# A two-layer cross-attention and feed-forward kernel: the second layer's queries made ahead of its loop for four batches and two heads at once, kept in DRAM, and one value phase a unit

## The reference

```
q_hk = (hidden_q @ Wq.T).reshape(Bv, Sv, H, K)               # 16 heads of 128
q_big = jnp.einsum('bshk,hkq->bshq', q_hk, w_kc_q)           # to 192
q_big = _apply_rope(q_big, sin_q[None, :, None, :], cos_q[None, :, None, :])
kv_r = _apply_rope(kv_c, sin_k[None], cos_k[None])           # 1444 rows of 64 a batch
q_r = jnp.einsum('bshq,hqr->bhsr', q_big, W_qr)              # to 64
k_r = jnp.einsum('bld,hdr->bhlr', kv_r, W_kr)
scores = jnp.einsum('bhsr,bhlr->bhsl', q_r, k_r)
attn = jax.nn.softmax(scores, axis=-1)
ctx_c = jnp.einsum('bhsl,bld->bhsd', attn, kv_r)
```

## Time and profile before

| | |
|---|---|
| three runs, us | 892.38, 897.06, 903.19 |
| profiled execution, its span from the first to the last instruction, us (the page has no time of its own for it beside this) | 903.0 |
| PE busy, us (share) | 826.4 (92%) |
| DVE, ACT, POOL busy, us | 585.3, 397.2, 453.2 |
| share of the chain that ended last on PE | 68% |
| first scores of the loop start, us | 306.13 |

### The profile page before, as it was taken

How to read it: one execution, slowest core, us unless ns; L and a number is a source line. 1 busy time by engine, 2 the same in 40 slices (tenths; PEclk the granted TensorE clock), 3 DMA queues, 4 the chain that set the end, 5 groups by cost and what they waited for, 6 DMA issues and landing times.

```text
span 903.0 us, 15604 instructions
## 1 busy us (share of the span) xinstructions
PE 826.4 (92%) x5844; PEld 606.6 (67%) x5844; DVE 585.3 (65%) x1133; ACT 397.2 (44%) x883; POOL 453.2 (50%) x465
## 2 busy tenths in 40 slices
PE   4998879999998799999999999999999999999883
PEld 3566656788887667677667677676767766765442
DVE  3437864213358675677878778778787787786545
ACT  2248852222231454544544454454354454444441
POOL 3000002800041187768776876776776776567630
PEclk9979996999999899999999999999999999999986
DMA  9532022789810100000000100000000000000000
GB/s 212 187 123 89 2 67 79 261 299 317 299 46 10 35 1 12 18 10 10 19 10 1 31 10 2 10 26 7 10 23 10 10 6 10 2 16 10 2 13 11
DMA packets 42168, 52.28 MB, mean 58 GB/s; under 512 B 12230, under 2 KB 35704, under 8 KB 41836
## 3 DMA queue, kind: packets, MB, share of 16 engines
q1 hardware_dynamic: 41068, 49.63, 17.5%
q0 software_dynamic: 1024, 1.64, 0.6%
HBM read 45.80 MB, written 5.36 MB: 57 GB/s over the span
## 4 chain that ended last, share of the span: by engine, by line
PE 68%; DVE 13%; ACT 7%; DMA 5%; issue 5%; SPq 1%; POOL 0%; POOLq 0%; ACTq 0%; DVEq 0%
PE ps L1197 14%; PE ps L1209 10%; PE ps L1177 7%; PE ps L1116 6%; PE ps L1121 3%; PE ps L1232 3%; DMA xs<-xs_scratch 3%; PE ps L1042 3%; PE ps L994 3%; PE ps L1143 3%; ACT sm L1465 2%; PE ps L1055 2%; DVE xyz L1947 2%; DVE xyz L1943 1%; PE ps L893 1%
## 5 line engine op out<-in xcount | busy, mean ns | idle before, releaser
L614 POOL TENSOR_TENSOR acc<-acc,pt 120x800 f32<-120x800 f32 (+1 forms) x157 | 299.1, 1905 | 94.4 <-ACT pt L1674 61.4
L1674 ACT ACTIVATE pt<-ps 120x400 f32<-120x400 f32 (+1 forms) x384 | 190.1, 505 | 222.5 <-PE ps L1197 211.6
L1976 DVE TENSOR_REDUCE nm<-ps 128x1 f32<-128x482 f32 (+1 forms) x336 | 213.7, 655 | 100.3 <-PE ps L1177 98.1
L1197 PE MATMUL ps<-qh,khl 128*120 128x400 f32 (+1 forms) x384 | 157.9, 411 | 11.1 <-ACT pt L1674 8.3
L1209 PE MATMUL ps<-pt,kv 120*64 120x400 f32 (+1 forms) x768 | 143.8, 510 | 0.0
L1177 PE MATMUL ps<-khl,qh 128*128 128x482 f32 (+1 forms) x336 | 131.6, 393 | 5.3 <-DVE nm L1976 4.6
L1197 PE MATMUL ps<-ql,kh 65*120 65x400 f32 (+1 forms) x384 | 134.3, 350 | 0.0
L1197 PEld LDWEIGHTS ps<-qh,khl 128*120 128x120 f32 (+1 forms) x384 | 70.9, 185 | 58.6 <-issue 32.4
L1209 PEld LDWEIGHTS ps<-pt,kv 120*64 120x64 f32 (+1 forms) x768 | 51.9, 138 | 65.8 <-issue 55.8
L636 POOL TENSOR_TENSOR rstd<-veps,mhalf 100x1 f32<-100x1 f32 (+2 forms) x20 | 13.4, 670 | 158.1 <-DVE veps L1808 114.6
L1197 PEld LDWEIGHTS ps<-ql,kh 65*120 65x120 f32 (+1 forms) x384 | 71.3, 186 | 5.1
(11 more groups left out here) (277 smaller groups left out, 1246.0 us busy)
## 6 DMA issues: line engine op xcount, KB each, us to landing
egu<-_L_ffn_gate_up_proj_dram SPq DMA_DIRECT2D x14, 1024.0 KB, 6.0
edn<-in_L_ffn_down_proj_dram SPq DMA_DIRECT2D x14, 512.0 KB, 7.1
spread<-inv_scratch SPq DMA_DIRECT2D x30, 100.0 KB, 2.7
craw<-in_ctx_dram SPq DMA_DIRECT2D x8, 360.0 KB
wo_n<-in_L_xattn_Wo_dram SPq DMA_DIRECT2D x1, 2048.0 KB, 10.5
wq_n<-in_L_xattn_Wq_dram SPq DMA_DIRECT2D x1, 2048.0 KB, 8.0
xs_scratch<-zero SPq DMA_DIRECT2D x1, 1792.0 KB, 9.9
xs<-xs_scratch SPq DMA_DIRECT2D x14, 128.0 KB, 6.1
```

What stands on the lines that cost most here:

```text
L614: nc.gpsimd.tensor_tensor(total[r, :, :], before[r, :, :], pt[j % PT_BUF][r, :, :], ALU.add).then_inc(p_added, 1)
L1197: last = mm(ps[0:key_rows(t), k % 2, 0:HT], lhs[:, keys], rhs[:, HT * a:HT * a + HT], start=first, stop=not first)
L1674: nc.scalar.activation(pt[j % PT_BUF][0:rows, k % 2, :], ps[0:rows, k % 2, 0:HT], ACT.Exp).then_inc(p_ready, 1)
L1976: nc.vector.tensor_reduce(nm3[0:w, i, n:n + 1], ps[0:w, 3 + m % 2, 0:MN], AX.X, ALU.max).then_inc(m_reduced, 1)
```

## The change

All queries of the second layer are made ahead of the loop. Sixteen steps `n` (two groups of four batches, eight pairs of heads) each make three products of 128 x 128 on 400 columns (`q_big`; the columns are four batches) in a ring of four PSUM banks, turn them on DVE (eight instructions of 400 columns), make `q_latent` in one bank, copy and subtract, and SP stores both halves in DRAM (`store_q`, four transfers a step, in pieces of 100 numbers). Inside the loop SP loads the queries of unit `u + 2` when the scores of unit `u` are done (`load_q`, three transfers of 200 KB). The first unit's 21 maximum pieces are spread over steps 8 to 14, three a step. All eight batches' layer norms (`third_input`, `norm_x3`), all six groups of ternary weights and all key rotations on POOL come ahead of the loop.

With the queries out of the loop, the buffers `pt` grow from 8 to 14, and a unit's 12 value tiles stand in one group behind slot 23, with `sum_weights` of the same unit behind them. `keep_sums` moves from slot 7 to slot 2 of the next unit and `invert_sums` from slot 9 to slot 7. The slots of the keys, of the output product and of the feed-forward parts stay.

```diff
+QG = 4
+QN = (B // QG) * GH
+QRING = (0, 1, 6, 7)
+FIRST_MAX_FROM, FIRST_MAX_EACH = 8, 3
-KEEP_AT, INVERT_AT, DIVIDE_AT = 1, 9, 15
+KEEP_AT, KEEP_SUMS_AT, INVERT_AT, DIVIDE_AT = 1, 2, 7, 15
-PT_BUF = 8
+PT_BUF = 14
...
+        def store_q(sp, n):
+            g, p, i = n // GH, n % GH // HG, n % HG
+            sp.wait_ge(q_lo, n + 1)
+            dst = q_dram.rearrange("(b p) k d (e i q) -> p k e i d b q", p=PAIRS, e=2, i=HG)
+            for e in range(2):
+                for k, src in ((0, qs_hi[n % 2]), (1, qs_lo[n % 2])):
+                    sp.dma_start(dst[p, k, e, i, :, QG * g:QG * g + QG, :],
+                                 src[CD * e:CD * e + CD, :].bitcast(F32).rearrange("d (b q) -> d b q", b=QG)).then_inc(q_stored[n % 2], 16)
+        def load_q(sp, u):
...
+            if u >= 2:
+                sp.wait_ge(s_done, LANE * (u - 1))
+            for k in range(2):
+                sp.dma_start(qh[u % 2][CD * k:CD * k + CD, :].bitcast(F32), q_dram[u, 0]).then_inc(q_loaded, 16)
+            sp.dma_start(ql[u % 2][0:CD, :].bitcast(F32), q_dram[u, 1]).then_inc(q_loaded, 16)
...
+            for n in range(QN):
+                store_q(sp, n)
+                if n % HG == HG - 1 and n < GH:
+                    load_q(sp, n // HG)
+                if n in KEYS_AT:
+                    load_keys(sp, 4 + KEYS_AT.index(n))
+            place_max(sp, 0)
...
+            def q_big(n, part):
+                g, h = n // GH, 2 * (n % GH)
+                m = 3 * n + part
...
+                if m >= 4:
+                    pe.wait_ge(rope_done, m - 3)
...
+                for c in range(DC):
+                    lhs = wqb[:, c, h + part, 0:128] if part < 2 else wqt[:, c, h:h + 2, :].rearrange("p h q -> p (h q)")
+                    last = mm(ps[:, QRING[m % 4], 0:HT], lhs, x3T[:, c, HT * g:HT * g + HT], start=c == 0, stop=c == DC - 1)
+                last.then_inc(qbig_done, 1)
...
+            for n in range(QN):
+                for part in range(3):
+                    q_big(n, part)
+                if n:
+                    q_latent(n - 1)
+                if 1 <= n <= QG:
+                    turn_x3(QG + n - 1)
+                for c in first_max(n):
+                    max_chunk(0, c)
+            q_latent(QN - 1)
             turn_max(0)
...
-                    if u + 2 < NU and f < 2 and x in QB_AT:
-                        for part in range(2):
-                            q_big(u + 2, f, 2 * QB_AT.index(x) + part)
...
-                    if x == PHASE - 1:
-                        if f == 2 and u + 2 < NU:
-                            q_latent(u + 2)
-                        for i in range(4):
-                            if f == 0 and u and i == 3:
-                                sum_weights(u - 1)
-                            values(KT * u + 4 * f + i)
+                    if at == LANE - 1:
+                        for t in range(KT):
+                            values(KT * u + t)
+                        if u < NU - 1:
+                            sum_weights(u)
...
+            for n in range(QN):
+                for part in range(3):
+                    rope(n, part)
+                if n:
+                    low_q(n - 1)
+                if n < QG:
+                    third_input(QG + n)
+                if 1 <= n <= QG:
+                    norm_x3(QG + n - 1)
...
+                for c in first_max(n):
+                    reduce_max(0, c)
```

More of the change, by code:

```diff
@@ L258, in build @@
         cursor[0] = after_keys
+        xn3 = [place(f"xn3{i}", [S, D]) for i in range(2)]
+        x3T = place("x3T", [128, DC, T])
+        assert cursor[0] <= after_qb
+        cursor[0] = after_keys
         eq = place("eq", [S, B, NE])
@@ L271, in build @@
         cursor[0] = after_qb
-        kv += [place(f"kv{i}", [KP, KT, CD]) for i in range(2, KV_BUF)]
+        kv += [place("kv2", [KP, KT, CD])]
         ctu = [place(f"ctu{i}", [128, HT]) for i in range(2)]
@@ L280, in build @@
         end_3 = cursor[0]
+        cursor[0] = sums_at
+        qs_hi = [place(f"qs_hi{i}", [128, HT], F32R) for i in range(2)]
+        qs_lo = [place(f"qs_lo{i}", [128, HT], F32R) for i in range(2)]
+        assert cursor[0] <= after_spread
+        q_dram = nc.dram_tensor("q_scratch", [NU, 2, CD, GQ], F32, kind="Internal").ap()
         after_stage = max(end_1, end_2, end_3)
@@ L425, in build @@
         sums_spread = sem("sums_spread")
+        q_stored, q_loaded = [sem(f"q_stored{i}") for i in range(2)], sem("q_loaded")
         inv_spread = sem("inv_spread")
@@ L700, in _ @@
             nc.gpsimd.memset(nm3[:, :, :], 0.0).then_inc(tails_set, 1)
-            pool.wait_ge(fq_turned, 6)
+            for b in range(2, B):
+                for j in range(KT // 2):
+                    rotate_keys(pool, step, b, j)
+                if b < QG:
+                    third_power(pool, power, QG + 2 * (b - 2))
+                    third_power(pool, power, QG + 2 * (b - 2) + 1)
             for b in range(B):
@@ new lines, in q_latent @@
+            def q_latent(n):
+                h = 2 * (n % GH)
+                pe.wait_ge(rope_done, 3 * n + 3)
+                if n:
+                    pe.wait_ge(q_lo, n)
+                else:
+                    pe.wait_ge(x_shared, B)
+                for j in range(3):
+                    for e in range(2):
+                        last = mm(ps[CD * e:CD * e + CD, 2, 0:HT], amat[:, h + e, j, :], xyz[n % 2][:, j, e, :], start=j == 0, stop=j == 2)
+                last.then_inc(q_done, 1)
@@ L1213, in sum_weights @@
             def sum_weights(u):
+                b, p = u // PAIRS, u % PAIRS
+                if u:
+                    pe.wait_ge(sums_kept, u)
+                if p and b:
+                    pe.wait_ge(gated, 2 * b)
                 pe.wait_ge(p_added, (KT - 1) * (u + 1))
-                pe.wait_ge(p_ready, min(LANE * (u + 1) + PHASE, SLOTS * B))
                 for a in range(2):
-                    last = mm(ps[CD * a:CD * a + CD, 0, 0:HT], ones[0:KP, :], acc[u % 2][:, a, :], start=True, stop=True)
+                    last = mm(ps[CD * a:CD * a + CD, 7, 0:HT], ones[0:KP, :], acc[u % 2][:, a, :], start=True, stop=True)
                 last.then_inc(sums_done, 1)
@@ L1623, in keep_sums @@
                     act.wait_ge(sums_spread, 32 * (u - 1))
-                keep(sums[u % 2][:, :], ps[0:CD + 1, 0, 0:HT]).then_inc(sums_kept, 1)
+                else:
+                    for i in range(2):
+                        act.wait_ge(q_stored[i], 64 * (QN // 2))
+                keep(sums[u % 2][:, :], ps[0:CD + 1, 7, 0:HT]).then_inc(sums_kept, 1)
             def keep_xq(b):
@@ L1680, in _ @@
                         keep_keys(b + 1, KEEP_KEY_SLOT.index(s))
[L1681 removed]
+                    if u and at == KEEP_SUMS_AT:
                         keep_sums(u - 1)
@@ L1952, in low_q @@
-            def low_q(u):
-                dve.wait_ge(q_hi, u + 1)
-                for a in range(2):
-                    cols = slice(HT * a, HT * a + HT)
-                    last = tt(ql[u % 2][0:CD, cols], ps[CD * a:CD * a + CD, 5, 0:HT],
-                              qh[u % 2][CD * a:CD * a + CD, cols].bitcast(F32), ALU.subtract)
-                last.then_inc(q_lo, 1)
+                dve.wait_ge(rstd3_ready, b + 1)
+                if b >= 2:
+                    dve.wait_ge(x3_turned, b - 1)
@@ new lines, in norm_x3, with over_batches, by_batch, rope @@
+                ts(xn3[b % 2][:, :], x_sb[:, b, :], mv[:, b, 0:1], rstd[:, b:b + 1], ALU.subtract, ALU.mult).then_inc(xn3_ready, 1)
+            def over_batches(table, rows):
+                return table.unsqueeze(1).to_broadcast([rows, QG, S])
+            def by_batch(v):
+                return v.rearrange("p (b q) -> p b q", b=QG)
+            def rope(n, part):
+                m = 3 * n + part
+                dve.wait_ge(qbig_done, m + 1)
+                if part == 0 and n >= 2:
+                    dve.wait_ge(q_done, n - 1)
+                o, src = xyz[n % 2], ps[:, QRING[m % 4], 0:HT]
+                for j in range(2):
+                    if part < 2:
+                        last = tt(by_batch(o[:, j, part, :]), by_batch(src), over_batches(ropeq[:, j, :], 128), ALU.mult)
+                    else:
+                        for e in range(2):
+                            half = slice(CD * e, CD * e + CD)
+                            last = tt(by_batch(o[CD * j:CD * j + CD, 2, e, :]), by_batch(src[half, :]),
+                                      over_batches(ropeq[half, 2 + j, :], CD), ALU.mult)
+                last.then_inc(rope_done, 1)
```

361 lines of the change are left out of this document (149 added, 212 removed).

## The result

The changed kernel takes 945.75 us (median of 4 runs) against 900.12 us for the kernel before (median of 4 runs, the earlier three among them); the ratio is 1.0528, 95% interval 1.0466 to 1.059. The change is a clear loss, about twice the one forecast (919 us), and the time lies above the range of 893 to 935. Of all executions one stands apart, in the first form of experiment 7: it took 2687.6 us where the other nine took 896.6 to 908.5; the cause is open, and the ratio given there leaves it out. The profiled execution has a span of 945.4 us, 42.4 more than the 903.0 of the one before.

What follows compares the result with a forecast made beforehand. PE was taken to bound the loop, idle only 1.9 us a batch. Applied to the median of 897.1 us, +97 ahead of the loop and -75 in it made +22: 919 us, range 893 to 935.

Steps and rivals of the forecast that it cites:

- the three terms: Start to first `q_big` +11 us, first `q_big` to first scores +86, first scores to the end -75.
- The failed step: Steps 0 to 3 ahead of the loop: DVE also makes the second group's norms, adding 1.6 us in all.
- the first part: Start to first `q_big`: ternary groups and the rest of the shared output move ahead, so it starts at about 277 us.
- Maximum pieces ahead of the loop: Steps 8 to 14: the third piece waits for DVE's subtraction and reduction, 2.4 us a step, 17 in all.
- The last stores ahead of the first scores: Behind the last step: copy, subtraction, turn, and four SP stores ahead of the maxima's two transfers, 7 us.
- The loop: First scores to the end: a middle batch takes 63.4 us, PE idling 8.0 where it idled 1.9; together -75 us.
- the price from the rows alone: PE work a batch loses in the loop through `q_big` pieces and `q_latent` of two units: 13.9 us.
- the 2.0 that I added for switches and `turn_x3`: Further PE work leaving a batch: about 0.9 us query switches, 0.8 value-group switches (both estimates), 0.3 `turn_x3`.
- The value phase "at nothing": Single value group per unit: its tiles cover POOL's sums, the maxima's row and the query loads, so it costs nothing.
- Covered slots: Rival: two banks either way absorb the loop's stops, a batch idles 1.9 and takes 57.3 us; 880 us, chance 0.15.
- Within 1%: Rival: idle of 3.5 to 6.1 us a batch, or the 17 us of maximum pieces hidden (902 us); chance 0.20.
- Stores as the bound: Rival: 400 B pieces take twice the mean, a step's stores 7.9 us, PE waits +14; 933 us, chance 0.10.

Runs made afterwards that it cites:

- the first form of experiment 7: Changed kernel with turned norms later, maximum pieces spread, keys in the value phase, first maxima placed before the last two stores: 904.0 us, ratio to before 1.0007.
- Experiment 1: Changed kernel with the second group's turned norms one step later on PE and ACT: 930.4 us, ratio to the kernel before 1.0285.
- experiment 2: Changed kernel with one maximum piece behind each `q_big` of steps 8 to 14, instead of three behind `q_latent`: 936.3 us, ratio to before 1.0383.
- experiment 3: Changed kernel with the values in three groups again, queries still ahead of the loop: 969.0 us, ratio to the kernel before 1.075.
- experiment 6: Changed kernel with three value groups and a third `qh` buffer, so queries load a unit earlier; 8 `pt` buffers: 937.8 us, ratio to before 1.0385.
- experiment 5: Changed kernel with twelve unread query-sized pieces a batch put back on PE at the old slots: 995.0 us, ratio to the kernel before 1.1019.

## Why the prediction was wrong

The direction, the reason (cover lost in the loop, little won by batching) and two of the three terms were right. One step failed.

- **The failed step:** "Steps 0 to 3 also give DVE the second group's norms, +1.6 in all." I counted the instructions as DVE's work beside PE's longer work, and did not ask who waits for them. `turn_x3` stands on PE one step too early, so the norm's place in DVE's queue sets the start of the next step. Steps 1 to 4 took 17.6 us more than the four steps of 6.6 us that the sum has with this term in it: 11.3 us of waits, and 5.9 us because PE came out of them at a lower clock. Experiment 1, which moves nothing else, gets these 17.6 us back. With them the sum is +40 instead of +22; the first part, 279.6 for 277, adds 2.6, and the profiled spans differ by 42.4.
- **Maximum pieces ahead of the loop:** held; 8.46 us a step where "about 8.6" was said, and experiment 2 shows that the wait was there for the order alone.
- **The last stores ahead of the first scores:** held; 6.6 us from the end of the last `q_latent` against 7, and the first form of 7 takes them away.
- **The loop:** -74.0 against -75, the batch 62.6 against 63.4. Its two halves were each off, against each other. PE's busy time fell from 71.4 to 57.6, by 13.8, which is the price from the rows alone (13.9); the 2.0 that I added for switches and `turn_x3` is not to be seen. The idle time came to 5.0, not 8.0: 3.9 in the even unit, where I had 5.5, and 1.1 in the odd one, where I had 2.5. The last batch and what follows it took 1.3 us more than before (93.3 from the start of its unit 14, for 92.0), where 3 less were forecast. That the sum fitted is luck in part.
- **The value phase "at nothing":** near nothing in the sum (PE waited twice for POOL's sums, which I had ruled out, 2.2 us in all), but wrong in its reason. I wrote that the queries loaded come "a whole unit early". They do not: the maximum pieces use them at the next slot 1, and only the single phase hides the load (31.3 us of waits in 13 units of experiment 3 without it). Against three groups with the load early it costs 7.0 us (experiment 6).
- **Covered slots (the rival on the other side):** fell; the waits on ACT and DVE are there, and experiment 5 shows that work in the slots is a quarter free.
- **Within 1%:** the idle time that this rival asked for came, 5.0 us a batch between its 3.5 and 6.1, but beside 57.6 us of PE's own work and not 55.4, and steps 1 to 4 took the time elsewhere. (From the prediction's own ends, 880 us with 1.9 of idle and 919 with 8.0, no change lies at 4.6 us of idle, not at 4.8.)
- **Stores as the bound:** fell. Steps 5 to 7 take 6.4 us with PE never waiting. The page's queue took 23.9% of sixteen engines' span, 3615 us, 1087 more than the earlier trace rows for 21,248 more packets: 51 ns each, below the mean of 61.6 that I used, and most of them are the 400 B pieces. They are smaller, though: 16.39 MB more, 771 B a packet for the 1208 B of the earlier trace rows, so a byte took 0.066 ns of an engine for 0.051. The rule that pieces under 512 B stay below line rate (the Trainium skill, DMA: Bandwidth & Descriptors, Specifications) agrees in its direction; no run shows its price alone, and at this load no step waited for it.

## What to carry to other kernels

When work is moved to a place where one engine feeds the next in steps, write down for each hand-over which instruction stands ahead of it in the giver's queue; a short instruction behind long ones costs the wait, not its length, and a turn of the order by one step can make it free. Work on the engine that bounds a loop also covers the others' work beside it, so price a removal by what will wait afterwards. And before a phase is called free, ask which transfer lies under it.

## What the runs showed of the hardware

A wait on PE can cost more than its length, and the surplus is not fixed. After the change, behind the wait of 4.28 us, the granted clock was 0.50 for 5.7 us, and the eight instructions that take 2.85 us at 1.00 took 5.59. Behind the two waits of 2.75 us they took 4.57 and 4.27, at 0.58 and 0.65 over the first 4.1 us; behind that of 1.53 us they took 2.88, at 1.00. In the four steps this came to 5.9 us on top of 11.3 us of waiting. In experiment 2, which has the same text there, waits of 3.97, 2.75, 2.75 and 1.80 us were followed by 4.18, 2.88, 4.32 and 2.88 us: 2.9 us on top of 11.3. A wait of 2.75 us was thus followed by anything from nothing to 1.7 us of loss.

Small store pieces were cheap by the packet and dear by the byte: from 330 to 420 us after the change, 14,080 packets of the main queue, 13,333 of all packets there under 512 B, took 36.1% of sixteen engines' time, 37 ns each for 519 B on average, where the kernel before had 61.6 ns for 1208 B.
